# The entry of an attention and mixture-of-experts kernel: constant matmuls while TensorE waits, finer waits, and copies moved to ScalarE

## The chip, the cores and the metric

One core of a Trainium2 chip runs the whole program. The metric is the device time of one execution in microseconds (us), lower is better.

## The reference

```
x:  [16, 512, 128] float32          # 16 batches of 512 tokens, 128 wide
xn = layernorm(x)
out = x + attention(xn) + experts(xn)

attention: q, k, v = xn Wq, xn Wk, xn Wv in 16 heads of 8; q and k scaled to length 1 per head
           softmax(8 q k^T, causal) v, then Wo
experts:   8 experts of 128 -> 512 -> 128 with gelu and biases; each token goes to the 2 experts
           with the highest router probability, weighted by those two probabilities made to sum to 1
```

## The kernel before

The program has these stages. **Stage A** (to about 75 us) normalises the 16 batches two at a time, turns them, and has TensorE compute for each token the router's logits and the raw q and k (`joint`); ScalarE squares those (`squares`), GpSimd sums the squares per head (`sum_squares`, L580), ScalarE takes the roots (`roots`, L770), all to scale q and k later. The **entry** (75 to 118 us) routes the tokens and starts attention; it is what the change touches. Then follow attention for batches 0 to 7, the expert tiles, and attention for batches 8 to 15, in which the expert results come back.

**Attention of one batch** is one `body` per engine, in an order written out by hand. TensorE goes through 12 units k (`scores`, L892): each fills 1536 columns of scores in one of two sets of three PSUM banks. ScalarE takes the exponential of each unit in one instruction (L812) into `prob`; TensorE may fill unit k+1 of scores only when the exponential of unit k-1 is done. GpSimd cuts off the causal part (`mask`, L657). TensorE weighs the values with the result in ten chunks (`weigh`, L926), five per half of the heads, into the one PSUM bank `ps_o` (bank 6); VectorE empties it with `evacuate` (L1349) after chunk 4 and after chunk 9. Chunk 5 waits for the first emptying.

**The next batch is prepared inside this one.** For each of the four 128-token tiles of batch b+1, TensorE computes q, k and v (`project`, L870, into bank 7), and VectorE runs `prepare`: `unload` scales q and k into `qn` and copies v (L1229), `halve` splits q and k into a 16-bit high part and remainder in `dup` (L1238, L1240) and copies both parts once more (L1245, L1246). When `dup_done` counts the tile, SP issues a DMA transpose into `qks` (`turn_qk`, L431). The first scores of a batch wait for all four transposes. TensorE can't project the next tile before VectorE has copied v of the last (`proj_evac`).

**Batch 0's own tiles** are prepared in the entry, into banks 0 to 3. `project(0, 2)` and `project(0, 3)` wait until ScalarE has read the last of the raw q and k.

**Routing.** VectorE's `select` finds the first and second expert of each token (`selected`). TensorE counts them with matmuls against ones and a residue mask (L985 to L994), and ranks every token in `ps_pc`, bank 7 (L997, L999; `placed`). VectorE turns counts into where each expert's rows begin, in some twenty small dependent steps, gives the position of the padding (`pad_ready`), turns ranks into slots and then counts `routed`:

```
            dve.memset(ps_o, 0.0).then_inc(r_step, 1)
            dve.wait_ge(r_step, next_step())
            dve.sem_inc(routed, 1)
```

Three places wait for `routed`: TensorE before `project(1, 0)` (it writes bank 7, where the ranks are) and before `weigh(0, 0, 0)` (it writes bank 6, where the counts are), and GpSimd before it moves the first rows to their slots. GpSimd's part of batch 0 is: first the indirect DMA that writes the padding rows (`pad_last_tiles`, L620, waits for `pad_ready`), then the masks, and from unit 5 on, once `routed` and the padding's landing (`padded`) are there, eight indirect DMAs (`move`, L650) spread over the masks of units 5 to 10.

SP's queue in the entry holds, in order: the transposes of batch 0, two loads of rows, the load of `xt` for batch 1, and the load of half of `acc` (2 MB).

ScalarE's order in the entry is: the last 8 `squares`, the last six roots (batches 10 to 15), the exponentials. GpSimd's sum for batch b waits until the roots of batch b-2 are taken, since `sums` has two buffers.

## Time and profile before

| | |
|---|---|
| median of 3 runs | 680.59 us (680.46 to 680.67) |
| the profiled execution's own time | 680.41 us |
| its span | 678.7 us |
| busy TensorE / VectorE / ScalarE / GpSimd | 615.8 / 465.7 / 449.9 / 418.0 us |
| mean granted TensorE clock | 0.975 of full |

The profile is of one execution; its times count from the start of the span. PE is TensorE, PEld its loading of weights, DVE VectorE, ACT ScalarE, POOL GpSimd, SPq SyncE's DMA queue. In the timeline a row merges instructions of one line that follow each other: start, us, engine, line, operation, how many, and in brackets the idle time before it and what ended it. The granted clock is 1.00 at 2.4 GHz and 0.50 at 1.2 GHz. "Issue" is idle time that ended with nothing the profile shows as a releaser.

### The profile page before, as it was taken

How to read it: one execution, taken by the hardware profiler on the slowest of the kernel's cores; microseconds unless marked ns; L12 is line 12 of the kernel's file. 1: busy time of each engine (PE TensorE's matmuls, PEld its weight loads, DVE VectorE, ACT ScalarE, POOL GpSimd, SP SyncE). 2: the span in 40 equal slices, each digit the busy share in tenths (PEclk: the TensorE clock that was granted, in tenths of full speed). 3: DMA queues.
4: the chain of work that ended last, by engine and by line, in shares of the span. 5: the costliest groups of instructions: out<-in, count | busy, mean ns of one | idle time of the engine just before them, and what ended most of it. 6: DMA issues, size and time to landing. Idle time of an engine off the chain costs nothing. (4 is left out here: it accounts for less than half of the span.)

```text
span 678.7 us, 21454 instructions
## 1 busy us (share of the span) xinstructions
PE 615.8 (91%) x7417; PEld 411.7 (61%) x7417; DVE 465.7 (69%) x1312; ACT 449.9 (66%) x689; POOL 418.0 (62%) x584
## 2 busy tenths in 40 slices
PE   2877558999999999999999999999999999999965
PEld 2755323444444438999999999999984444444423
DVE  7799986766676776445545446777566687878826
ACT  3999546888888884444444444444449888888854
POOL 6355627778777787775600027677737777677771
PEclk9899968999999999999999999999999999999989
DMA  5997685655445578855432335444536375556621
GB/s 160 297 288 228 185 248 111 109 108 104 115 115 118 125 126 199 206 143 143 108 88 71 73 88 120 112 115 118 120 78 104 84 137 116 121 124 139 122 68 32
DMA packets 186592, 89.36 MB, mean 132 GB/s; under 512 B 115456, under 2 KB 176032, under 8 KB 186400
## 3 DMA queue, kind: packets, MB, share of 16 engines
q1 hardware_dynamic: 178192, 70.70, 44.7%
q0 software_dynamic: 8336, 17.84, 9.8%
q8 instruction: 36, 0.59, 0.4%
q14 instruction: 28, 0.23, 0.1%
HBM read 30.17 MB, written 32.24 MB: 92 GB/s over the span
## 5 line engine op out<-in xcount | busy, mean ns | idle before, releaser
L812 ACT ACTIVATE prob<-psum 128x1536 f32<-128x1536 f32 x192 | 267.2, 1453 | 64.0 <-PE psum L922 62.2
L822 ACT ACTIVATE prob<-psum,prob 128x256 f32<-128x256 f32 x284 | 117.5, 471 | 132.2 <-PE psum L1062 129.3
L648 POOL DMA_INDIRECT rows<-slot_y,idx x128 | 130.4, 1019 | 46.1 <-issue 27.2
L650 POOL DMA_INDIRECT slot_x<-rows,slots x128 | 128.2, 1001 | 36.1 <-issue 30.4
L954 PE MATMUL psum<-prob,v 128*18 128x448 f32 (+3 forms) x2048 | 137.9, 388 | 8.6 <-POOL prob L664 8.6
L664 POOL TENSOR_SCALAR_AFFINE_SELECT prob<-prob 128x384 f32<-128x384 f32 (+2 forms) x224 | 104.8, 477 | 62.6 <-ACT prob L812 60.5
L1074 PEld LDWEIGHTS psum<-prob 128*128 128x128 f32 x1136 | 137.8, 192 | 3.6
L1074 PE MATMUL psum<-prob 128*128 128x128 f32 x1136 | 138.1, 275 | 0.0
L1062 PE MATMUL psum<-xs,prob 128*128 128x256 f32 x568 | 134.8, 380 | 0.6 <-DVE xs L1468 0.4
L1062 PEld LDWEIGHTS psum<-xs,prob 128*128 128x128 f32 x568 | 102.5, 190 | 12.4 <-DVE xs L1468 0.6
L954 PEld LDWEIGHTS psum<-prob,v 128*18 128x18 f32 x2048 | 48.8, 98 | 97.0 <-issue 75.9
L922 PE MATMUL psum<-qks 32*128 32x192 f16 (+3 forms) x1024 | 74.2, 276 | 2.5 <-ACT prob L812 2.4
L1475 DVE TENSOR_TENSOR xs<-psum,prob 128x256 f32<-128x256 f32 x71 | 30.1, 425 | 52.5 <-PE psum L1074 52.5
L882 PE MATMUL psum<-wall,xt 128*128 128x384 f32 x128 | 58.5, 541 | 3.6 <-issue 3.1
L1452 DVE COPY prob<-wexp 128x516 f32 x71 | 31.4, 443 | 38.0 <-ACT prob L822 34.6
L922 PEld LDWEIGHTS psum<-qks 32*128 32x128 f16 x1024 | 22.1, 92 | 42.4 <-ACT prob L812 17.4
L1460 DVE COPY prob<-wexp 128x640 f32 x71 | 35.8, 505 | 14.8 <-DVE xs L1475 14.5
L1397 DVE SCALAR_TENSOR_TENSOR acc<-rows,gate,acc 128x128 f32<-128x128 f32 (+1 forms) x128 | 42.7, 398 | 1.4 <-DVE acc L1381 0.8
L633 POOL COPY idx<-slots 128x8 int32 (+1 forms) x16 | 3.7, 231 | 63.8 <-PE psum L1074 63.6
L1240 DVE TENSOR_TENSOR dup<-qn,dup 128x256 f16<-128x256 f32 x64 | 36.3, 567 | 2.2
L1222 DVE TENSOR_TENSOR qn<-psum,rnb 128x256 f32<-128x256 f32 x36 | 14.8, 412 | 31.1 <-PE psum L882 31.0
L845 PE MATMUL psum<-wall,xts 128*128 128x264 f32 x128 | 32.3, 399 | 4.2 <-ACT logits L767 4.2
(159 smaller groups left out, 661.3 us busy)
## 6 DMA issues: line engine op xcount, KB each, us to landing
slot_y<-xs SPq DMA_DIRECT2D x71, 128.0 KB
xs<-in_L_attn_x SPq DMA_DIRECT2D x16, 256.0 KB, 4.1
prob<-in_L_ffn_W SPq DMA_DIRECT2D x16, 256.0 KB, 3.6
xn_rows<-prob SPq DMA_DIRECT2D x16, 256.0 KB, 2.7
xn_cols<-xts SPq DMA_DIRECT2D x16, 256.0 KB, 3.0
xt<-xn_cols SPq DMA_DIRECT2D x16, 256.0 KB
rows<-xn_rows SPq DMA_DIRECT2D x16, 256.0 KB, 3.5
out<-acc SPq DMA_DIRECT2D x15, 256.0 KB
```

Source lines behind the costliest of these rows:

```text
L648: pool.indirect_dma_start(rows[:, j, c, t, :], None, done, where).then_inc(moved[j], 16)
L650: pool.indirect_dma_start(slot_x, where, halves_of_rows[:, j, 0, t, :], None).then_inc(moved[j], 16)
L664: pool.affine_select(out=p, in_=p, compare_op=ALU.is_ge, fill=0.0, base=HP, pattern=[[0, n], [0, 2], [1, HP]], channel_multiplier=-1).then ...
L812: act.activation(prob[:, KEPT[k], :], score[k % 2], ACT.Exp, scale=SCALE / UP ** 2)\
L822: act.activation(hs[:, s, c, :], psum[:, 2 * s + c // 2, (c % 2) * FT:(c % 2 + 1) * FT], ACT.Gelu, bias=ws[:, s, B1C + c:B1C + c + 1]).the ...
L882: pe.matmul(bank[:, 0:3 * D], xt[:, t * P:(t + 1) * P], wall[:, E:WEND], start=True, stop=True)\
L922: mm = pe.matmul(s[:, j * N + col:j * N + col + cols], keys, queries(qks[g:g + 32, par, 0, slab], kt, first, cols), start=True, stop=True)
L954: mm = pe.matmul(queries(ps_o[32 * g:32 * g + VW], kt, first, cols), pairs[par][:, kt * H // 2 + QH * o + g, odd:odd + VW], prob[:, KEPT[u ...
L1062: mm = pe.matmul(psum[:, 2 * s + c // 2, (c % 2) * FT:(c % 2 + 1) * FT], ws[:, s, c * P:(c + 1) * P], xgt[:, s, :], start=True, stop=True)
L1074: mm = pe.matmul(psum[:, 4 + s, j * D:(j + 1) * D], hs[:, s, c, j * P:(j + 1) * P], ws[:, s, W2C + c * D:W2C + (c + 1) * D], start=(c == 0 ...
L1240: dve.tensor_tensor(dup[:, t, :, :, 3 * DH:4 * DH], whole_qk, dup[:, t, :, :, 0:DH], ALU.subtract)\
L1397: dve.scalar_tensor_tensor(out=a, in0=r, scalar=gate[:, c, at(TB * m + t)], in1=a, op0=ALU.mult, op1=ALU.add).then_inc(combined, 1)
```

## The change

In seven parts:

1. TensorE: 24 matmuls of the constant `identh` with the constant `barred` (512 columns each) into bank 7, whose result nobody reads, before the wait for `selected`; six more into a bank of scores after the last weighing of batch 0.
2. TensorE: batch 0 has an order of its own, `first_batch`. `weigh(0, 0, 0)` comes after unit 3 instead of 4, the projections of batch 1 after units 4, 8, 9 and 11 instead of 3, 5, 7 and 8. The first two units of scores stand, as before, behind the ranks.
3. `routed` is split: `counts_read` releases `weigh(0, 0, 0)`, `ranks_read` releases `project(1, 0)`, and `routed` is left to GpSimd alone. VectorE's memset of `ps_o` goes.
4. ScalarE takes from VectorE, for batch 0, the copy of v and the two copies within `dup` (`share_first`): 12 instructions.
5. ScalarE takes the roots of batches 10 and 11 ahead of the last squares, and those of 12 to 15 between and behind its copies.
6. VectorE: the bias copy stands ahead of the last selection instead of behind it, `share_values(0, 0)` ahead of the counts; in batch 0 `evacuate(0, 0)` stands ahead of tile 2 of batch 1 instead of behind all tiles and `pick_tiles`.
7. GpSimd: the padding's DMA stands behind the masks of units 0 and 1 instead of ahead of them.

```diff
@@ gpsimd, body
-                if known(b, 0):
-                    pad_last_tiles()
                 for k in range(UN):
                     mask(b, k)
+                    if known(b, 0) and k == 1:
+                        pad_last_tiles()
@@ scalar
             stage_a(act, step)
+            roots(NB // 2 - 3)
             for s in range(2):
                 squares(NB // 2 - 1, 1, s)
-            for i in range(NB // 2 - 3, NB // 2):
-                roots(i)
+
+            def share_first(t):
+
+                act.wait_ge(qn_done, t + 1)
+                to = v[:, 0, t * H:(t + 1) * H, 0:DH].rearrange("p (m j) d -> p j m d", j=2)
+                act.copy(to, psum[:, t, 2 * D:3 * D].rearrange("p (j m d) -> p j m d", j=2, d=DH)).then_inc(proj_evac, 1)
+                act.wait_ge(lo_done, t + 1)
+                q_to = dup[:, t, 0].rearrange("p h (c d) -> p h c d", d=DH)
+                k_to = dup[:, t, 1].rearrange("p h (c d) -> p h c d", d=DH)
+                act.copy(q_to[:, :, 1:3, :], q_to[:, :, ::-3, :])
+                act.copy(k_to[:, :, 1:3, :], k_to[:, :, ::3, :]).then_inc(dup_done, 1)
+            act.wait_ge(made, 3)
+            for t in range(TB):
+                share_first(t)
+                if t < 2:
+                    root(NB - 4 + t)
+            for b in range(NB - 2, NB):
+                root(b)
@@ tensor, project
                     if i == 0 and known(b, 1):
-                        pe.wait_ge(routed, 1)
+                        pe.wait_ge(ranks_read, 1)
@@ tensor, weigh
                     if known(b, 0):
-                        pe.wait_ge(routed, 1)
+                        pe.wait_ge(counts_read, 1)
@@ tensor, entry
+            def keep_going(bank, n):
+
+                pattern = barred[:].rearrange("p (a c) -> p a c", a=1).broadcast_to([P, 2 * TB, HP])
+                for _ in range(n):
+                    pe.matmul(bank, identh[:], pattern, start=True, stop=True)
+            keep_going(ps_pc, 24)
             pe.wait_ge(selected, T // ST)
...
             pe.wait_ge(proj_evac, TB)
+            scores(0, 0, 0)
+            scores(0, 0, 1)
+
+            def first_batch():
+
+                for k in range(2, UN):
+                    scores(0, 0, k)
+                    if k == 3:
+                        weigh(0, 0, 0)
+                    elif k == 4:
+                        project(1, 0)
+                    elif k in (5, 6, 7):
+                        weigh(0, 0, k - 4)
+                    elif k == 8:
+                        project(1, 1)
+                    elif k == 9:
+                        weigh(0, 0, 4)
+                        project(1, 2)
+                    elif k == 10:
+                        weigh(0, 0, 5)
+                        weigh(0, 0, 6)
+                    elif k == 11:
+                        project(1, 3)
+                        weigh(0, 0, 7)
+                        pe.wait_ge(exp_done, UN - 1)
+                        keep_going(score[0][:, 0:N], 6)
@@ vector, unload and halve, batch 0
+                if known(b, 0):
+                    return
...
+                if known(b, 1) and i == 0:
+                    dve.wait_ge(dup_done, TB)
@@ vector, entry
-            for c in range(TOPK):
-                select(T // ST - 1, c)
             dve.wait_ge(btr_done, 1)
             dve.tensor_copy(wexp[:, :, B1C:W2C], psum[:, 5, 0:E * MC].rearrange("p (e c) -> p e c", e=E))\
                 .then_inc(bt_ready, 1)
+            for c in range(TOPK):
+                select(T // ST - 1, c)
+            share_values(0, 0)
...
             stepped(dve.tensor_copy(counts[:], ps_o[:, 0:2 * E].rearrange("p (c e) -> p c e", c=2)))
+            dve.sem_inc(counts_read, 1)
...
             stepped(dve.tensor_tensor(at_rank, ranks, of_halves(begins[:, 0:2]), ALU.add))
+            dve.sem_inc(ranks_read, 1)
...
-            dve.memset(ps_o, 0.0).then_inc(r_step, 1)
-            dve.wait_ge(r_step, next_step())
             dve.sem_inc(routed, 1)
@@ vector, body
                     prepare(b + 1, 1 - par, 1, second)
+                    if known(b, 0):
+                        evacuate(0, 0)
                     prepare(b + 1, 1 - par, 2, second)
```

How the instructions stand now, at three places. First TensorE in batch 0, from unit 3 of scores on (`qks` are scores, `wall,xt` a projection, `prob,xts` the weighing of chunk 0). Before:

```order
L922 MATMUL psum<-qks 128x448 [waits exp_done]
L922 MATMUL psum<-qks 128x448 x2
L922 MATMUL psum<-qks 128x64 x3
L882 MATMUL psum<-wall,xt 128x384 [waits proj_evac,routed,xt_in]
L922 MATMUL psum<-qks 128x320 [waits exp_done]
L922 MATMUL psum<-qks 128x320 x2
L922 MATMUL psum<-qks 128x192 x3
L943 MATMUL psum<-prob,xts 18x64 [waits exp_done,vp_ready,routed,proj_evac]
L943 MATMUL psum<-prob,xts 18x64 x15
```

And now:

```order
L944 MATMUL psum<-qks 128x448 [waits exp_done]
L944 MATMUL psum<-qks 128x448 x2
L944 MATMUL psum<-qks 128x64 x3
L965 MATMUL psum<-prob,xts 18x64 [waits exp_done,vp_ready,counts_read,proj_evac]
L965 MATMUL psum<-prob,xts 18x64 x15
L944 MATMUL psum<-qks 128x320 [waits exp_done]
L944 MATMUL psum<-qks 128x320 x2
L944 MATMUL psum<-qks 128x192 x3
L904 MATMUL psum<-wall,xt 128x384 [waits proj_evac,ranks_read,xt_in]
```

The weighing has moved ahead of unit 4, the projection behind it, and neither names `routed`. Second, TensorE at the end of batch 0, from unit 11 on, where nothing but a weighing stood between these scores and the next batch's first row (`barred,identh` waiting for the transposes):

```order
L944 MATMUL psum<-qks 128x320 [waits exp_done]
L944 MATMUL psum<-qks 128x320 x2
L944 MATMUL psum<-qks 128x192 x3
L904 MATMUL psum<-wall,xt 128x384 [waits proj_evac]
L976 MATMUL psum<-prob,v 18x448 [waits masked]
L976 MATMUL psum<-prob,v 18x448 x3
L976 MATMUL psum<-prob,v 18x64 x4
L1009 MATMUL psum<-barred,identh 128x512 [waits exp_done]
L1009 MATMUL psum<-barred,identh 128x512 x5
L928 MATMUL psum<-barred,identh 128x512 [waits qk_turned3,qk_turned2,exp_done,qk_turned1,qk_turned0]
```

The last projection of batch 1 now stands behind the last unit of scores, and the six constant matmuls behind the weighing. Third, ScalarE between its last square and its first exponential, where before only six roots stood:

```order
L812 COPY v<-psum 128x2x8x8 [waits qn_done,made]
L816 COPY dup<-dup 128x16x16 [waits lo_done]
L817 COPY dup<-dup 128x16x16
L778 ACTIVATE norms<-rows 128x128 [waits ss_ready]
L812 COPY v<-psum 128x2x8x8 [waits qn_done]
```

Each tile's three copies come in this order, the roots of batches 12 and 13 behind tiles 0 and 1.

## Rows read from the trace of the kernel before

**Rows 1.** The page, part 1: busy time and share of the span.

```profile
PE 615.8 (91%) x7417; PEld 411.7 (61%) x7417; DVE 465.7 (69%) x1312; ACT 449.9 (66%) x689; POOL 418.0 (62%) x584
```

**Rows 2.** Stretches: length, busy us (count) of PE, PEld, DVE, ACT, POOL; PEclk; DMA; GB/s.

```profile
80.00:82.00 2.00, 0.00 (x0) 0.00 (x0) 1.90 (x6) 0.31 (x1) 1.73 (x3) 0.96 0.94 232
...
94.00:96.00 2.00, 0.60 (x12) 0.12 (x6) 1.90 (x4) 2.00 (x2) 1.62 (x3) 0.87 1.05 289
...
112.00:114.00 2.00, 1.06 (x36) 1.01 (x40) 1.93 (x5) 1.16 (x1) 1.69 (x3) 0.64 0.91 173
...
118.00:138.00 20.00, 19.45 (x353) 8.51 (x343) 14.48 (x37) 16.87 (x12) 14.38 (x23) 1.00 0.58 110
```

**Rows 3.** Timeline of ACT, batches 0, 1 and 8: start, us, engine, line, operation [idle before].

```profile
92.31 5.48 ACT L812 ACTIVATE prob<-psum 128x1536 f32<-128x1536 f32 x4 [6.89 <-PE psum L922]
...
118.43 5.48 ACT L812 ACTIVATE prob<-psum 128x1536 f32<-128x1536 f32 x4 [0.75 <-PE psum L922]
...
509.52 10.93 ACT L812 ACTIVATE prob<-psum 128x1536 f32<-128x1536 f32 x8 [3.28 <-PE psum L922]
...
525.51 1.45 ACT L812 ACTIVATE prob<-psum 128x1536 f32<-128x1536 f32 x1 [0.25 <-PE psum L922]
```

**Rows 4.** Waits of PE, 60 to 125: total us, times, longest.

```profile
PE psum L985 <- DVE gap L1135: 9.6, 1, 9.6
...
PE psum L882 <- issue: 3.1, 1, 3.1
...
PE psum L943 <- DVE turn L1355: 2.5, 1, 2.5
```

**Rows 5.** Timeline of DVE, 72 to 87.

```profile
72.69 0.42 DVE L1222 TENSOR_TENSOR qn<-psum,rnb 128x256 f32<-128x256 f32 x1
...
81.62 1.14 DVE L1121 TENSOR_TENSOR mark<-logits,top 128x128 f32<-128x128 f32 x1
...
84.77 0.29 DVE L1121 TENSOR_TENSOR mark<-spent,top 128x128 f32<-128x128 f32 x1
...
86.28 0.17 DVE L1135 TENSOR_TENSOR gap<-top 128x16 f32<-128x16 f32 x1
```

**Rows 6.** Timeline of DVE and POOL in batch 0.

```profile
100.59 0.42 DVE L1222 TENSOR_TENSOR qn<-psum,rnb 128x256 f32<-128x256 f32 x1
...
102.05 0.22 DVE L1246 COPY dup<-dup 128x256 f16<-128x256 f16 x1
...
104.77 0.98 POOL L650 DMA_INDIRECT slot_x<-rows,slots  x1 [0.25 <-issue]
```

**Rows 7.** Timeline of PE, 75 to 118.

```profile
75.15 1.56 PE L882 MATMUL psum<-wall,xt 128*128 128x384 f32 x4 [0.53 <-ACT logits L767]
...
76.64 0.24 PE L980 MATMUL psum<-identf,b1n 32*128 32x32 f32 x1
...
90.17 1.06 PE L906 MATMUL psum<-barred,identh 128*128 128x512 f16 x2
...
113.77 1.93 PE L954 MATMUL psum<-prob,v 128*18 128x448 f32 x16
...
117.09 0.60 PE L906 MATMUL psum<-barred,identh 128*128 128x512 f16 x2
```

**Rows 8.** Timeline of ACT and POOL, 64 to 76.

```profile
64.95 1.05 ACT L757 COPY prob<-xns 128x1024 uint16<-128x1024 uint16 x1
...
73.77 0.39 ACT L766 ACTIVATE prob<-psum 128x256 f32<-128x256 f32 x1
...
75.45 0.40 POOL L601 TENSOR_TENSOR rows<-rows 128x128 f32<-128x128 f32 x1 [3.87 <-ACT norms L773]
```

**Rows 9.** DMA issues, 60 to 125: KB each, us to landing.

```profile
qks<-dup SPq DMA_TRANSPOSE x9, 3.6
...
acc<-in_L_attn_x SPq DMA_DIRECT2D x1, 0.5 KB, 11.8
...
slot_x<-acc,pad_at POOLq DMA_INDIRECT x1, 7.8
```

More of the change, by code:

```diff
@@ L253, in build @@
         r_step, counted, totals_read, placed = sems("r_step counted totals_read placed")
-        routed = sem("routed")
+        routed, counts_read, ranks_read = sems("routed counts_read ranks_read")
         residue_ready, later_ready = sems("residue_ready later_ready")
@@ L774, in roots, with root @@
                         .then_inc(norms_ready, 1)
+            def root(b):
+                act.wait_ge(ss_ready, b + 1)
+                act.activation(norms[:, TB * b:TB * (b + 1), :], sums[:, b % 2], ACT.Sqrt, scale=1.0 / UP ** 2)\
+                    .then_inc(norms_ready, 1)
             def step(i, par, j):
@@ L1019, in body @@
                         if not last:
[L1020 removed]
+                            project(b + 1, 1)
                     elif k == 4:
```

26 lines of the change are left out of this document (13 added, 13 removed).

## The prediction

> **What bounds the kernel now.** I read the page first: TensorE is busy for 91% of the span [rows 1], so most of the program is out of reach of an edit to its entry. The table by stretches shows the same for a settled stretch of attention: 19.45 of 20 us at granted clock 1.00, the higher level, 2.4 GHz [rows 2]. The change touches none of that code; it can only move the moment from which this regime runs. So I read the exponentials of ScalarE (one per unit of scores) in the timeline: the first of batch 0 starts at 92.31, the first of batch 1 at 118.43 [rows 3]. Batch 0 thus lasts 26.1 us, while batch 8, which enters with its operands ready, needs 16.0 us from its first to its last exponential [rows 3]. The room is there, and before it.
>
> TensorE's waits name three holes [rows 4]: 9.6 us for `selected` (VectorE's top-2 selection), 3.1 us before a projection ("issue": it is the wait for `routed`, the end of VectorE's routing), and 2.5 us for VectorE to empty the accumulator of batch 0. In their wake the granted clock is at or falls to 0.50, that is 1.2 GHz [rows 2]: the first hole starts at 76.88 [rows 7], and the row of 80 to 82 still has 0.96; the third starts near 110.5, and the row of 112 to 114 has 0.64. All later work is counted from semaphores, none from the clock on the wall, so I take what batch 1 starts earlier as what the program ends earlier.
>
> **Part 1: until `selected`.** The last selection op ends at 86.45 [rows 5]. VectorE loses twelve copies of batch 0, 0.22 to 0.28 us each [rows 6], some 0.7 per tile. Tiles 0 and 1 take from 72.69 [rows 5] to about 75.3 instead of 76.1. Tiles 2 and 3 can't start before their projection, which is behind ScalarE's squares (75.15, 1.56 for two [rows 7]); they end near 79.7 instead of 81.4. With 0.2 for the bias copy, now ahead, selection starts at 80.0 instead of 81.3. The selection itself took 5.1 us because GpSimd was still summing squares: the same comparison costs 1.14 then and 0.29 later [rows 5]. GpSimd loses 3.87 us at 75.45 to a root that ScalarE put behind the squares [rows 8]; the change moves that root ahead and interleaves the next ones, so GpSimd ends its sums about 3.7 us earlier, near 80.0. The selection then takes 4.0, twice the quiet half. `selected`: 84.0, **2.4 earlier**.
>
> The Trainium skill, SBUF — State Buffer, on the shared port pair, says that a GpSimd operation and certain VectorE operations exclude each other for the whole instruction; it agrees in direction with 1.14 against 0.29, but the step above needs only those two rows.
>
> ScalarE takes the copies. A 256-element activation is 0.39 [rows 8]; I take 0.3 + 0.39 + 0.39 = 1.1 per tile, tile 3 done at about 80.7, so its transpose (landing 3.6 after issue [rows 9]) is there at 84.4, before TensorE asks at 87. Bounds for one copy: 0.22, VectorE's own, and 1.05, a 1024-element ScalarE copy [rows 8]; I take 0.39 because size and type are nearest. SP's queue behind the transposes (rows, xt, acc) keeps its order.
>
> **Part 2: from `selected` to the first exponential.** Before: 86.45 to 92.31, 5.9 us, at the low clock. Two bias matmuls show the price of the level: 1.06 at 90.17 against 0.60 at 117.09 [rows 7]. The 24 added matmuls run from 76.9; at 0.27 to 0.30 each (half of that 0.60) they end by 83.4 to 84.1, at most 0.1 after `selected`. At the low level, 0.53 each, they would end at 89.6. The clock is high when they start (0.96 even in 80 to 82 [rows 2]), so I take the first. `share_values`, two copies on VectorE, hides under the counting matmuls. Ranks and first scores at the high clock: 5.9 becomes about 4.3, **1.6 earlier**. First exponential: 88.3.
>
> **Part 3: batch 0.** `weigh(0, 0, 0)` now needs only `counts_read` (about 86.5) and comes after unit 3; `project(1, 0)` needs `ranks_read`, two 512-element ops after the padding position, about 91.7, and is due at 92.8: the 3.1 us hole is gone, no wait takes its place. VectorE finishes routing near 95.9, without the memset and with `share_values` already done, and can take tile 0 of batch 1 at 97.2; before it was 100.59 [rows 6]. The evacuation of the first half moves ahead of tiles 2 and 3 and of `pick_tiles`, so TensorE's 2.5 us hole goes too. Exponentials follow batch 8's pace: 16.0 us from first to last.
>
> What is late next is GpSimd. Its padding transfer moves behind the mask of unit 1 (about 92) and took 7.8 us to land, against an acc load in flight that took 11.8 [rows 9]. The acc load now starts some 3 us sooner, so I take 6.5: padded at 98.5, while mask 5 is through at 97.6. Between 97.6 (no wait) and 101 (7.8, and the read in its way again). Then eight moves of 0.98 plus 0.2 to 0.3 [rows 6] and seven masks hold the masks of units 8 and 9 to about 105 and 108; I charge 1.5 us: last exponential at 88.3 + 16.0 + 1.5 = 105.8.
>
> From there the path to batch 1 is: `project(1, 3)`, now only behind unit 11, 0.8 plus 0.1; VectorE's preparation, 100.59 to 102.27 = 1.7 [rows 6]; SP 0.1; landing 3.6 [rows 9]; two bias matmuls and the scores, 117.09 to 118.43 = 1.3 [rows 7, 3]. Sum 7.6, so 113.4 against 118.43 [rows 3]: 5.0 earlier. TensorE meanwhile has one weighing (about 1, half of 1.93 [rows 7]) and the six added matmuls (1.6), then is idle for about 2.3 us; before, it lost the clock after some 2 us of idling (0.64 in 112 to 114 [rows 2]). A fall costs the first scores 0.8 (2.1 instead of 1.3) and up to another 1.0 in a batch in which TensorE has no slack. Nothing to 1.8; I take 1.2.
>
> **Sum:** 5.0 − 1.2 = 3.8 us off the profiled execution's 680.41 gives 676.6; the median of the runs shown is 680.59, 0.18 above it, so I forecast **676.8**. A difference of 0.2%, 1.4 us, is about what a measurement of this kernel can tell.
>
> **Rivals.**
> *No stall and no fall of the clock.* Padding lands before it is asked for and the two charges (1.5 and 1.2) vanish: 680.6 − 6.5 = 674.1. For it: the added matmuls stand exactly in the two largest holes. Against it: the 3.6 us landing behind a late `project(1, 3)` is plain. Chance 0.2.
> *The clock falls again within batch 0.* Right after the dense start, units 2 and 3 leave TensorE 0.4 us of work in each 1.35 us of ScalarE, and the hole around `selected` leaves it idle for 1 to 2 us. In the trace such a stretch was followed by a fall (0.87 in 94 to 96 [rows 2]). It would cost first the ranks and scores (1.6, the gain of part 2), later the weighings, 1.93 a chunk at the low level [rows 7], of which half would be saved at the high one, some 1 us more: 676.8 + 2 = 678.8, up to 679.6. Chance 0.25.
> The Trainium skill, TensorE: Matmul & The Clock Gate, A second HAM failure mode, says that a TensorE that idles briefly between groups of matmuls swings between the two levels. That rule speaks against batch 0 keeping the clock, as this rival has it; the sum without the rule is 676.8, with it 678.8.
> *Gain is taken back downstream* (GpSimd's moves or SP's loads set the start of batch 1 or 2, whatever VectorE does): within 1.4 us of 680.6. For it: eight moves are issued in batch 0 on the same engine as the masks. Against it: TensorE is full to 19.45 in 20 us from 118 on [rows 2], so it, and not GpSimd, sets the pace there. Chance 0.06.
> *Slower: ScalarE's copies.* They are strided, half from the 16-bit tile. The queue is ScalarE's: two of the last roots, then the table load and the first exponential stand behind them, and SP's transposes, with the acc load behind those. At 1.05 each, twelve copies and two roots end at 75.0 + 13.2 = 88.2; the last transpose lands at 91.9, the first exponential is at 93.4, 1.1 late; the acc load starts near 91 and shares the padding's time (97 + 11.8, the longest landing seen), so mask 9 is at 118 and batch 1 starts at about 120.5: 682.5. It decides from about 0.95 us per copy on. Chance 0.06.
>
> **The numbers.** My forecast, 0.43; no stall 0.2; clock falls 0.25; taken back 0.06; slower 0.06. The range reaches from the no-stall case, 674.1, to the worst of the falling clock, 679.8. Faster by over 0.2% (below 679.2): 0.43 + 0.2 + most of 0.25 = 0.86; same 0.07, slower 0.07.
>
> **What would show it.** `selected` near 84 with comparisons of 0.3 us; the 24 matmuls over by then; granted clock 1.00 through 76 to 92; first exponential at 88.3; no "issue" wait before a projection; GpSimd's first move at 98 to 99; first exponential of batch 1 at 113 to 115. The forecast is wrong if ScalarE's copies exceed 0.6 us, if the row around 84 to 90 reads 0.50, if padding holds GpSimd to 101, or if batch 2 starts less early than batch 1 does.

## The result, and the profile after

The changed kernel takes **684.91 us** (median of 14 runs, 680.88 to 688.09); the kernel before, on the same chip, 680.76 us (14 runs, 680.04 to 682.39). The ratio is 1.0055, 95% interval 1.0034 to 1.0077: slower by half a per cent, where 0.6% faster was forecast. The profiled execution is the slowest of the 14, 688.09 us with a span of 685.3, against 680.41 and 678.7 before; a place that it shows as late need not be as late in the median run.

The page, part 1, of the changed kernel [rows 1]:

```profile
PE 629.8 (92%) x7447; PEld 416.4 (61%) x7447; DVE 464.0 (68%) x1299; ACT 452.9 (66%) x701; POOL 416.6 (61%) x584
```

TensorE is busy 14.0 us longer, though the 30 added matmuls are only 5.35 + 1.47 us of it.

ScalarE's timeline, its first copies and the exponentials [rows 3]:

```profile
75.88 0.43 ACT L816 COPY dup<-dup 128x256 f16<-128x256 f16 x1
...
91.68 6.82 ACT L834 ACTIVATE prob<-psum 128x1536 f32<-128x1536 f32 x5 [6.83 <-PE psum L944]
...
110.58 1.45 ACT L834 ACTIVATE prob<-psum 128x1536 f32<-128x1536 f32 x1 [1.69 <-PE psum L944]
118.14 1.45 ACT L834 ACTIVATE prob<-psum 128x1536 f32<-128x1536 f32 x1 [6.12 <-PE psum L944]
...
140.37 2.79 ACT L834 ACTIVATE prob<-psum 128x1536 f32<-128x1536 f32 x2 [0.76 <-PE psum L944]
```

Batch 0 starts 0.63 us earlier than before, batch 1 0.29 earlier (118.14 against 118.43), batch 2 already 2.0 **later** (140.37 against 138.34), and from batch 2 to the end of the span it takes 544.9 instead of 540.4 us. 2.0 + 4.5 is the whole difference of the spans (6.6), and in this execution most of it arises in code that the change does not touch. (The two executions differ by 7.7 us; the other 1.1 lies outside the spans.)

Stretches of the changed kernel [rows 2]:

```profile
80.00:82.00 2.00, 2.00 (x11) 0.92 (x10) 1.83 (x4) 0.88 (x3) 1.86 (x4) 1.00 0.93 317
...
86.00:88.00 2.00, 0.78 (x11) 0.52 (x12) 1.54 (x6) 0.00 (x0) 0.00 (x0) 0.86 0.91 207
88.00:90.00 2.00, 2.00 (x6) 0.71 (x5) 1.60 (x11) 0.00 (x0) 0.00 (x0) 0.50 1.03 306
...
96.00:98.00 2.00, 2.00 (x16) 0.64 (x8) 1.77 (x4) 2.00 (x2) 1.94 (x3) 0.50 1.00 313
...
118.00:120.00 2.00, 2.00 (x38) 0.75 (x36) 0.00 (x0) 1.45 (x1) 0.28 (x1) 0.54 0.00 0
...
118.00:138.00 20.00, 20.00 (x291) 8.03 (x289) 12.73 (x36) 15.63 (x11) 12.36 (x20) 0.83 0.49 91
...
630.00:632.00 2.00, 2.00 (x37) 1.13 (x36) 0.00 (x0) 1.78 (x2) 0.43 (x2) 0.54 0.03 8
```

TensorE's timeline [rows 7]:

```profile
77.56 5.35 PE L1009 MATMUL psum<-barred,identh 128*128 128x512 f16 x24
86.40 0.40 PE L1014 MATMUL psum<-ones,both 128*128 128x128 f16 x4 [3.49 <-DVE gap L1190]
...
89.89 1.06 PE L928 MATMUL psum<-barred,identh 128*128 128x512 f16 x2
...
110.46 0.91 PE L904 MATMUL psum<-wall,xt 128*128 128x384 f32 x2
112.24 1.06 PE L976 MATMUL psum<-prob,v 128*18 128x448 f32 x16 [0.86 <-POOL prob L664]
113.23 1.47 PE L1009 MATMUL psum<-barred,identh 128*128 128x512 f16 x6
116.82 0.59 PE L928 MATMUL psum<-barred,identh 128*128 128x512 f16 x2 [2.12 <-issue]
```

The 24 constants run at the high level, 0.22 us each, and are over at 82.9. Then TensorE has nothing until 86.40, the clock falls to 1.2 GHz near 87.3, and the ranks and bias matmuls run at the old price (1.06). It is low again in 94 to 100, during batch 0. The waits for routing and for the first emptying are gone. The last projection starts at 110.46; the last exponential of batch 0 at 110.58, where before it was 116.22. But batch 1 can't start before the last tile's transpose, and from 110.58 to 118.14 pass 7.6 us; of these 2.12 are a hole behind the six constants. Right behind it the clock falls, and batch 1 runs its first 6 us at the low level: 22.23 us instead of 19.91.

VectorE and GpSimd, timeline of the changed kernel [rows 5, 8, 6]:

```profile
78.44 1.28 DVE L1295 CAST dup<-qn 128x256 f16<-128x256 f32 x1
...
82.42 0.28 DVE L1174 TENSOR_REDUCE top<-logits 128x16 f32<-128x128 f32 x1
82.73 0.29 DVE L1176 TENSOR_TENSOR mark<-logits,top 128x128 f32<-128x128 f32 x1
...
86.18 0.17 DVE L1190 TENSOR_TENSOR gap<-top 128x16 f32<-128x16 f32 x1
...
78.30 1.27 POOL L594 TENSOR_TENSOR rows<-prob 128x512 f32<-128x512 f32 x1 [0.17 <-POOL rows L601]
...
95.53 1.21 POOL L623 DMA_INDIRECT slot_x<-acc,pad_at  x1 [0.47 <-issue]
...
102.57 0.98 POOL L650 DMA_INDIRECT slot_x<-rows,slots  x1 [1.61 <-issue]
```

and the same pair before:

```profile
76.64 0.80 DVE L1238 CAST dup<-qn 128x256 f16<-128x256 f32 x1
...
76.02 1.27 POOL L594 TENSOR_TENSOR rows<-prob 128x512 f32<-128x512 f32 x1 [0.17 <-POOL rows L601]
```

GpSimd did end its sums earlier (80.8 instead of 83.8), and the selection behind them is quick (0.29 a comparison). But the same sums now start almost with VectorE's casts. A cast takes 0.28 alone; here it ends 0.15 us after the sum does, whenever it began: before at 77.44 against 77.29, now at 79.72 against 79.57. The first selection step is at 82.42, not at 80.0.

### The profile page after: what moved, and what is told of

It is laid out like the page before. It is cut to its first block and busy times, and to the rows that moved or that the text cites. A ratio compares the mean times of both kernels' runs of the same rounds, so it can differ in the third digit from the quotient of the medians.

```text
span 685.3 us, 21517 instructions
## 1 busy us (share of the span) xinstructions
PE 629.8 (92%) x7447; PEld 416.4 (61%) x7447; DVE 464.0 (68%) x1299; ACT 452.9 (66%) x701; POOL 416.6 (61%) x584
## 5 line engine op out<-in xcount | busy, mean ns | idle before, releaser
L664 POOL TENSOR_SCALAR_AFFINE_SELECT prob<-prob 128x384 f32<-128x384 f32 (+2 forms) x224 | 103.4, 471 | 78.5 <-ACT prob L834 64.6
L976 PE MATMUL psum<-prob,v 128*18 128x448 f32 (+3 forms) x2048 | 139.9, 393 | 10.6 <-POOL prob L664 10.4
L1129 PEld LDWEIGHTS psum<-prob 128*128 128x128 f32 x1136 | 137.8, 192 | 3.6
L944 PE MATMUL psum<-qks 32*128 32x192 f16 (+3 forms) x1024 | 75.6, 280 | 2.8 <-ACT prob L834 2.7
L904 PE MATMUL psum<-wall,xt 128*128 128x384 f32 x128 | 60.0, 554 | 0.5 <-ACT logits L767 0.5
```

The lines of the kernel that those rows point to most:

```text
L664: pool.affine_select(out=p, in_=p, compare_op=ALU.is_ge, fill=0.0, base=HP, pattern=[[0, n], [0, 2], [1, HP]], channel_multiplier=-1).then ...
L904: pe.matmul(bank[:, 0:3 * D], xt[:, t * P:(t + 1) * P], wall[:, E:WEND], start=True, stop=True)\
L944: mm = pe.matmul(s[:, j * N + col:j * N + col + cols], keys, queries(qks[g:g + 32, par, 0, slab], kt, first, cols), start=True, stop=True)
L976: mm = pe.matmul(queries(ps_o[32 * g:32 * g + VW], kt, first, cols), pairs[par][:, kt * H // 2 + QH * o + g, odd:odd + VW], prob[:, KEPT[u ...
L1129: mm = pe.matmul(psum[:, 4 + s, j * D:(j + 1) * D], hs[:, s, c, j * P:(j + 1) * P], ws[:, s, W2C + c * D:W2C + (c + 1) * D], start=(c == 0 ...
```

## The experiments

All times are medians of 6 to 14 runs, beside runs of the kernel before on the same chip; its median there was 679.7 for a1 to a4 and 680.2 to 680.8 for the others. The ratio and its interval are against those runs; the ratio is an estimate of its own and differs from the quotient of the medians by up to 0.3%. From each profile I take three starts, the first exponentials of batches 0, 1 and 2 (b0, b1, b2), and "rest", the span minus b2. These come from one execution each, which can be far from the median: d4's profile is 7.3 us below it, c3's 2.1 below, c4's 2.2 and the changed kernel's 3.2 above. "Added" is the number of TensorE matmuls more than before; each is two instructions, a weight load and a matmul. No kernel leaves out part of the computation; the constant and small matmuls write what nobody reads. The theories are numbered in the order in which I formed them: **theory 5** is that the number of added instructions moves the loading of TensorE's instructions against the later batches; **theory 6** that the padding's transfer shares its time with the `acc` load and so holds GpSimd's first move and batch 0.

| kernel | added | b0 | b1 | b2 | rest | median | ratio (95%) |
|---|---|---|---|---|---|---|---|
| before | 0 | 92.31 | 118.43 | 138.34 | 540.4 | 680.8 | |
| changed | 30 | 91.68 | 118.14 | 140.37 | 544.9 | 684.9 | 1.0055 (1.0034–1.0077) |
| a1_no_constant | 0 | 91.29 | 118.76 | 141.12 | 541.4 | 683.8 | 1.0052 (1.0030–1.0074) |
| a2_end_16 | 40 | 92.05 | 121.37 | 141.28 | 543.4 | 684.5 | 1.0064 (1.0041–1.0087) |
| a3_start_38 | 44 | 89.69 | 120.32 | 142.49 | 552 | 686.4 | 1.0093 (1.0057–1.0129) |
| a4_project_early | 30 | 92.09 | 117.87 | 137.79 | 543.4 | 683.9 | 1.0056 (1.0033–1.0078) |
| b1_pad_first | 30 | 91.36 | 117.60 | 137.51 | 544.9 | 686.0 | 1.0098 (1.0080–1.0116) |
| b2_pad_project | 30 | 91.55 | 118.14 | 138.05 | 543.5 | 684.4 | 1.0063 (1.0046–1.0081) |
| b3_copies_back | 30 | 93.11 | 119.63 | 139.54 | 542.8 | 685.5 | 1.0104 (1.0066–1.0141) |
| b4_before_split | 0 | 92.89 | 119.46 | 139.37 | 538.6 | 678.7 | 0.9973 (0.9952–0.9993) |
| c1_before_30 | 30 | 92.59 | 119.00 | 138.91 | 545.4 | 684.3 | 1.0053 (1.0031–1.0076) |
| c2_before_128 | 128 | 92.59 | 118.81 | 138.72 | 540.1 | 680.3 | 0.9989 (0.9976–1.0003) |
| c3_after_128 | 128 | 91.71 | 120.44 | 139.69 | 541.7 | 685.2 | 1.0062 (1.0042–1.0082) |
| c4_project_128 | 128 | 90.11 | 121.09 | 141.01 | 540.5 | 681.1 | 1.0004 (0.9989–1.0019) |
| d1_split_late_acc | 0 | 92.62 | 119.18 | 139.03 | 540.5 | 679.7 | 0.9981 (0.9959–1.0003) |
| d2_project_128_late | 128 | 89.14 | 112.49 | 132.38 | 540.3 | **675.9** | 0.9932 (0.9912–0.9953) |
| d3_project_none_late | 0 | 92.05 | 116.28 | 138.95 | 540.7 | 681.8 | 1.0020 (1.0006–1.0034) |
| d4_after_late_acc | 30 | 91.27 | 116.56 | 136.47 | 542.3 | 687.8 | 1.0124 (1.0102–1.0147) |
| e1_project_late_30 | 30 | 92.10 | 116.72 | 136.63 | 545.2 | 682.7 | 1.0031 (1.0008–1.0054) |
| e2_after_128_late | 128 | 89.68 | 115.85 | 138.70 | 539.2 | 678.4 | 0.9979 (0.9961–0.9997) |

Read the column "rest" first. With 0 or 128 added it is 538.6 to 541.7 in ten profiles, with 30 it is 542.3 to 545.4 in eight, with no overlap; with 40 (a2) it is 543.4. (a3's profile, 696.35 us, lies 10 us above its median, and its row is not used for this.)

One place separates the kernels more sharply than "rest" does. Batch 13 lasts 19.0 to 20.0 us in the ten profiles with 0 or 128 added, and 20.8 to 21.5 in the ten with 30, 40 or 44 (a3's counted here). TensorE's idle time just before batch 14 is at most 0.92 us in the first ten and 1.76 to 2.26 in the others.

Of the expectations below, those of b4, c1, c2, e1 and e2 were met in the median, and d2's within 0.1 us. The medians of a2 to a4, b1, b2, c3, c4, d1, d3 and d4 fell outside what the theory under test gave; those of a1 and b3 decide little.

**Constants: none, more at the end, more at the start.**

```diff
@@ a1_no_constant
-            keep_going(ps_pc, 24)
-                        pe.wait_ge(exp_done, UN - 1)
-                        keep_going(score[0][:, 0:N], 6)
@@ a2_end_16
-                        keep_going(score[0][:, 0:N], 6)
+                        keep_going(score[0][:, 0:N], 16)
@@ a3_start_38
-            keep_going(ps_pc, 24)
+            keep_going(ps_pc, 38)
```

> The changed kernel without its 24 + 6 constant matmuls. Theory 1 (the loss is the fall of TensorE's clock at the start of batch 1, which lasts 22.2 us instead of 19.9): without the six the idle stretch before batch 1 is longer still, the clock falls there or before, batch 1 starts no later; about the same as the changed kernel, 684 to 687. Theory 2 (the constant matmuls themselves hold up work): faster than the changed kernel by over 1 us.

> The changed kernel with 16 instead of 6 constant matmuls behind the last weighing of batch 0, so that TensorE is busy until the transposes of batch 1 have landed. Theory 1 (fall of the clock): batch 1 runs at 1.00 and lasts about 19.9 us instead of 22.2, the median falls by 2 us or more, to 682 or 683, and the runs scatter less. Rival (the start of batch 1 is bound by something else and the clock costs nothing): no change, or up to 1 us slower where the ten added matmuls outlast the transposes.

> The changed kernel with 38 instead of 24 constant matmuls ahead of the selection (about 8.5 us instead of 5.4, from 77.5 to 86.0, with selected at 86.3). If the clock that fell at 87.3 is what kept the first exponential at 91.7, it starts at about 90.2 now and batch 1 up to 1.5 us earlier: 683 to 684. If the start of batch 1 is bound by the late projection and GpSimd's masks, the first exponential moves and batch 1 does not.

Without constants "rest" is 3.5 shorter and b2 0.75 later, and the median is 683.8, as good as with them: they gain nothing where they stand. It also shows that the changed kernel is slower than the one before (1.0052) without a single added matmul; of the 3.8 us between those two spans, 2.8 lie ahead of batch 2. Sixteen at the end bridge the wait for the transposes, and batch 1 keeps its clock (19.91 us), but batch 0 is longer and the sum is no better. Thirty-eight at the start reach `selected`, and b0 comes 2 us earlier; batch 0 then takes 30.6 us instead of 26.5. That is from the profile set aside above, but c4 shows the same in an ordinary one (31.0). Something else held batch 0.

**The projections of batch 1 earlier; the padding's DMA first; both.**

```diff
@@ a4_project_early
                     elif k in (5, 6, 7):
                         weigh(0, 0, k - 4)
+                        if k == 7:
+                            project(1, 1)
                     elif k == 8:
-                        project(1, 1)
-                    elif k == 9:
                         weigh(0, 0, 4)
                         project(1, 2)
                     elif k == 10:
+                        project(1, 3)
                         weigh(0, 0, 5)
                         weigh(0, 0, 6)
                     elif k == 11:
-                        project(1, 3)
                         weigh(0, 0, 7)
@@ b1_pad_first
+                if known(b, 0):
+                    pad_last_tiles()
                 for k in range(UN):
                     mask(b, k)
-                    if known(b, 0) and k == 1:
-                        pad_last_tiles()
@@ b2_pad_project: both
```

> The changed kernel with the projections of tiles 1, 2 and 3 of batch 1 after units 7, 8 and ahead of the chunks of unit 10 (instead of after units 8, 9 and 11), and weighing of chunk 4 after unit 8. Theory 2 (batch 1 starts late because its last tile is projected behind the last unit of scores, at 110.5): the last transpose is issued 2 to 3 us earlier, TensorE's idle time before batch 1 goes, batch 1 starts at about 116 and keeps the clock: 681 or less. Theory 1 alone gives the same gain by the clock. Rival (GpSimd's masks behind its moves set the end of batch 0): no change.

> The changed kernel with the padding's DMA back ahead of the mask of unit 0. Theory 3 (GpSimd sets the end of batch 0: its first row move waits for the padding to land, 102.5 in the changed kernel, and the masks of units 7 to 9 stand behind the moves): padding is issued at 93 instead of 95.5, the first move stands at 100 to 101, batch 1 starts 1.5 to 2 us earlier, and, as TensorE idles less before it, may keep its clock: 681 to 683. Rival (late projection, theory 2): first move earlier, batch 1 unchanged, 684 to 685.

> Both the padding first and the projections early. If both bounds count, batch 1 starts about 3 us before the 118.1 of the changed kernel, near 115, and lasts 19.9: 680 to 681. If one of them is the bound, no better than the better of the two alone.

With the last projection behind unit 10 the hole before batch 1 is filled and b2 is at 137.8, 2.6 us before the changed kernel's, yet the median moves by 1 us: "rest" is still 543.4. Issuing the padding first gains nothing: its landing goes from 6.3 to 9.1 us, and the first move comes at 102.2 instead of 102.6. Together they are no better.

**ScalarE's copies and roots undone; the split of the waits alone.** b3 is the changed kernel with the last six roots behind the squares, and VectorE's 12 copies back. b4 is the kernel before with only parts 3 and 6 of the change (less the reordering of `evacuate` and the bias copy):

```diff
@@ b4_before_split
-                        pe.wait_ge(routed, 1)
+                        pe.wait_ge(ranks_read, 1)
...
-                        pe.wait_ge(routed, 1)
+                        pe.wait_ge(counts_read, 1)
...
+            share_values(0, 0)
             dve.wait_ge(btr_done, 1)
...
-            dve.memset(ps_o, 0.0).then_inc(r_step, 1)
-            dve.wait_ge(r_step, next_step())
```

> The changed kernel with the twelve copies of batch 0 back on VectorE and the roots back behind the squares. Theory 4 (the earlier roots put GpSimd's sums beside VectorE's casts, so these cost 1.28 instead of 0.28, and moving copies gains nothing before selected): selected no later than in the changed kernel, time the same. If moving the copies did gain the 0.8 us that the trace shows against the last squares, selected is that much later and the time 0.5 to 1 us more.

> The kernel before with only the split of the routing's wait (counts, ranks), share_values ahead of the counts and no memset. TensorE's 3.1 us wait before the first projection goes. If that wait was on the path, batch 0 is shorter by up to 3 us and the time is 678 to 679. If the landing of the padding (101) takes its place, since GpSimd then reaches unit 5 before it, batch 0 is shorter by 1 to 2 us at most: within 1 us of the kernel before.

b3's `selected` is late by what the copies had gained:

```profile
87.25 0.61 PE L997 MATMUL psum<-ones,both 128*128 128x128 f16 x4 [4.35 <-DVE gap L1173]
```

0.85 us after 86.40, and b0 1.4 later; the median is 0.5 us above the changed kernel's, and the ratio 1.0104 against 1.0055, with intervals that overlap. So parts 4 and 5 do no harm; whether they help in the total is not shown. The split alone is the first version that is faster than before, by 0.27%, and its "rest" is not longer.

**The number of instructions by itself.** The kernel before, with small matmuls in its 9.6 us wait for `selected`:

```diff
@@ c1_before_30 (c2_before_128: 128)
+            for _ in range(30):
+                pe.matmul(psum[0:32, 7, 0:HP], identh[:, 0:32], barred[:], start=True, stop=True)
             pe.wait_ge(selected, T // ST)
@@ c3_after_128, the changed kernel (c4_project_128: the same on a4)
-            keep_going(ps_pc, 24)
+            keep_going(ps_pc, 20)
+            for _ in range(102):
+                pe.matmul(psum[0:32, 7, 0:HP], identh[:, 0:32], barred[:], start=True, stop=True)
```

> The kernel before with 30 small matmuls (32 weights columns, 64 columns, result unread) in TensorE's 9.6 us wait for the selection; they take some 1 to 2 us of it. Theory 5 (the change's 30 added matmuls, 60 instructions with their weight loads, shift where the later program's instruction fetches, 16 KB each in the DMA rows, fall, so that some fall beside the transposes at a batch's end and cost up to 2 us more where the clock then falls): the time from the start of batch 2 to the end rises from 540.4 by 2 us or more, as in every kernel that holds the constant matmuls (542.8 to 552), with batch 2 at 20.2 or more instead of 19.46 and batch 13 at 20.8 or more instead of 19.78; median 682 or more. Rival (the later losses of the changed kernel come from when batch 1 starts, or from ScalarE's and GpSimd's order): 680.2, within 0.5, like the kernel before.

> The same with 128 small matmuls: 256 instructions of 64 bytes, just one fetch of 16 KB. Theory 5: every later fetch falls where it did, one further on, so from batch 2 on as in the kernel before (540.4), batches 2 and 13 at 19.5 and 19.8; median within 1 us of before, or a little faster as the clock falls later in the wait. Rival (any added matmuls cost later): as the one with 30.

> The changed kernel with 20 + 102 small + 6 = 128 added matmuls instead of 24 + 6. Theory 5: from the start of batch 2 on 540.4 instead of 544.9; the entry unchanged or up to 1 us later: 681 to 682. Rival: 684 to 686 as the changed kernel.

> The same in the kernel with the projections early, whose batch 2 began at 137.8 (1.3 us earlier than in the kernel before, counted from the last squares). Theory 5: 679 to 680, beating the kernel before by about 1 us. Rival: 683 to 684 as without it.

These runs show what the count does to the kernel before. Thirty matmuls, 1.05 us of work hidden in a wait of 9.6, make the old kernel **3.5 us slower**, 1.0053, near the ratio of the whole change. A hundred and twenty-eight of them, 3.91 us of work in the same wait, cost nothing. The fetching of instructions has rows of its own in the DMA part of the page: the larger of two queues named "instruction" has 36 packets, 0.59 MB, so 16 KB each, and I take it to be TensorE's. How many instructions one carries I can only estimate. Ten intervals between fetches span the 73 us from 117 to 190 in the kernel before, in which TensorE starts 2,546 loads and matmuls: some 255 for each. The queue then fetches nothing from 190 to 234, from 263 to 499 and from 562 to 607, where the program goes again through loops of two batches or two expert tiles. That 256 is a whole number of pieces was a guess that led to the run, and the fetches agree with it. From 117 to 190 they fall into the microseconds 117, 125, 132, 138, 146 before, and into 117, 126, 132, 139, 147 with 128, which has one more fetch, at 81, in the wait itself; with 30 it is 115, 122, 129, 137, 146. Around batch 8, whose first exponentials are at 509.52, 509.57 and 510.92, they fall into 510, 517 and 526 before and with 128 as well, but into 510, 517 and 527 with 30, against the batch some 1.4 us earlier at the first two. c1 loses 0.4 us in batch 2 (19.85 against 19.46), 0.8 in batch 8, 1.5 in batch 13 and 2.4 in batch 14, where nothing was changed.

Where part of it is lost can be seen at the end of batch 13. Timeline of SP and TensorE, the last transpose's issue and the next batch's first matmul. Before:

```profile
619.69 1.24 SPq L431 DMA_TRANSPOSE qks<-dup  x1
...
624.72 0.59 PE L906 MATMUL psum<-barred,identh 128*128 128x512 f16 x2 [0.73 <-ACT prob L812]
```

c2, with 128:

```profile
619.25 1.24 SPq L431 DMA_TRANSPOSE qks<-dup  x1
...
624.21 0.59 PE L906 MATMUL psum<-barred,identh 128*128 128x512 f16 x2 [0.67 <-ACT prob L812]
```

c1, with 30:

```profile
621.58 1.24 SPq L431 DMA_TRANSPOSE qks<-dup  x1
...
627.91 0.59 PE L906 MATMUL psum<-barred,identh 128*128 128x512 f16 x2 [2.00 <-issue]
```

and the changed kernel:

```profile
622.43 1.23 SPq L431 DMA_TRANSPOSE qks<-dup  x1
...
628.50 0.59 PE L928 MATMUL psum<-barred,identh 128*128 128x512 f16 x2 [1.80 <-issue]
```

From issue to first row 5.0 and 5.0 us without or with 128, 6.3 and 6.1 with 30. TensorE idles 2.0 and 1.8 us instead of 0.7. In these two kernels the clock then falls: the stretch 630 to 632 above has 0.54 and batch 14 takes 22.2 us in the changed kernel and 21.7 in c1, against 19.3 and 19.4. But the wait is not enough for the fall. a2 waits longest of all but one, keeps 1.00, and its batch 14 takes 19.4; a4, b2, b3 and d4 keep it too, after 1.76 to 2.13 us. Timeline and stretch of a2:

```profile
630.76 0.59 PE L928 MATMUL psum<-barred,identh 128*128 128x512 f16 x2 [2.25 <-issue]
```

```profile
632.00:634.00 2.00, 2.00 (x40) 0.82 (x38) 0.00 (x0) 1.92 (x2) 0.34 (x2) 1.00 0.14 41
```

Shown is that the loss hangs on the count, and that a part of it arises in the wait ahead of batch 14, where the program asks for the transposes. What lengthens the wait is not shown. That an instruction fetch delays the transpose was my inference, and the traces do not bear it out. Behind the issue of the last transpose the larger instruction queue fetches after 4.3, 2.7, 3.2 and 2.5 us (before, c2, c1, changed), which does not set the slow pair apart. The packets of the hardware DMA queue run off alike before and in c1: 3.3 us behind the issue 8,641 and 8,602 are still to come. Only the changed kernel lags, with 8,700. A rival that I did not test is that TensorE itself runs short of instructions there: its idle time ends with "issue" in both late kernels, that is with nothing that the profile shows as a releaser.

c3 and c4 have "rest" back at 541 and still don't win: their batch 0 takes 28.7 and 31.0 us. c4's median is 2.8 us below a4's, but c3's, 685.2, is the changed kernel's own, and is where the rival had put it: in the order of the changed kernel the right count alone gains nothing. Part of why is in c3's profile. Its constants end 1.30 us before the ranks, and the clock falls all the same, so that the ranks cost 1.91 and b0 is no earlier (91.71):

```profile
86.44 0.40 PE L1016 MATMUL psum<-ones,both 128*128 128x128 f16 x4 [1.30 <-DVE gap L1192]
...
88.22 1.91 PE L1030 MATMUL psum<-turn,xs 128*128 128x512 f16 x4
```

c4, timeline of GpSimd and its DMA landings:

```profile
105.98 0.98 POOL L650 DMA_INDIRECT slot_x<-rows,slots  x1 [6.87 <-issue]
```

```profile
acc<-in_L_attn_x SPq DMA_DIRECT2D x1, 0.5 KB, 17.2
slot_x<-acc,pad_at POOLq DMA_INDIRECT x1, 11.2
```

The earlier `selected` brings padding and `acc` load together: 11.2 us to land instead of 6.3, and GpSimd stands still for 6.87. That is theory 6.

**The `acc` load behind the loads for batch 2.** SP issues it after the `xt` of batch 2, instead of in the entry:

```diff
@@ d1 to d4, e1, e2
-            load_acc(0, T // 2)
...
                         load_xt(b + 2)
+                    if known(b, 0):
+                        load_acc(0, T // 2)
```

d1 is b4 with it, d2 is c4, d3 is a4 without any constants, d4 is the changed kernel; e1 is a4 with its 30 constants, e2 is c3.

> The kernel before with the split waits, share_values ahead, no memset, and the load of half of acc behind the transposes and the xt load of batch 0's body. Theory 6 (padding behind the acc load bounds batch 0 once the waits are split): padding lands in 4 to 6 us, the first move stands at 100 or before instead of 103.4, batch 1 starts 1 to 2 us earlier than 119.5: 677 to 678. Rival (batch 0 there is bound by TensorE at the low clock): as the split alone, 678.7.

> The changed kernel with early projections, 128 added matmuls and the late acc load. Theory 5 and 6: first move at 98 to 100 instead of 106, batch 0 24 to 25 us instead of 31, batch 1 at 115 to 116, from batch 2 on 540.4: 676 to 677.5. If only theory 5 holds, 681 as without the late load.

> The same with no constant matmuls at all. Fetches in place as in the kernel before; what is missing is only the clock they keep. Theory: the first exponential 0.5 to 1.5 us later than in the one with 128, batch 1 possibly at the low clock (22 instead of 19.9): 677 to 680.

> The changed kernel with only the late acc load. Theory 6: first move at 99 to 100 instead of 102.6, batch 1 about 2 us earlier; theory 5: from batch 2 on still 543 to 545: 682 to 683. Rival to theory 5 (the later loss comes from something the late entry causes): back to 679.

> The changed kernel with the projections of batch 1 earlier and the acc load behind batch 2's xt, with its 24 + 6 constant matmuls and none added to make them 128. It differs from the fastest version so far (675.9, 128 added matmuls) only in that number. Theory of the instruction count: the entry is as good as that one's (batch 2 starts within 1 us of 132.4 minus what four more constants in the entry give or take), but from batch 2 to the end it takes 542 to 545 instead of 540.3, so the median is 679 to 683. Rival, that the 128 matter only by keeping TensorE busy in the entry: batch 2 starts 3 to 5 us later, and from batch 2 to the end it takes 540 to 541. Rival, that the count does not matter at all: 675 to 677.

> The changed kernel with its own order of projections, 128 added matmuls (20 constants, 102 small, 6 constants) and the acc load behind batch 2's xt. It differs from the fastest version so far only in the order of projections. Theory: batch 0 is 1 to 3 us longer than that one's 23.35, because the last projection stands behind unit 11, TensorE waits 2 us for the transposes behind the six constants and batch 1 begins at the low clock (22 instead of 19.9); from batch 2 to the end 540 to 542; median 678 to 681. Rival, that the order of projections is worth nothing once the number of instructions is right and the padding lands early: 675 to 677.

**d2 beats both kernels, 675.9 us.** It differs from c4 in the `acc` load alone: the padding lands in 4.8 us, batch 0 goes from 31.0 to 23.4. Timeline of d2, ScalarE, TensorE and GpSimd:

```profile
89.14 10.85 ACT L835 ACTIVATE prob<-psum 128x1536 f32<-128x1536 f32 x8 [5.33 <-PE psum L945]
...
112.49 5.48 ACT L835 ACTIVATE prob<-psum 128x1536 f32<-128x1536 f32 x4 [4.19 <-PE psum L945]
...
80.91 3.15 PE L1013 MATMUL psum<-barred,identh 128*32 128x64 f16 x102
85.35 0.40 PE L1017 MATMUL psum<-ones,both 128*128 128x128 f16 x4 [1.29 <-DVE gap L1193]
...
86.95 1.02 PE L1031 MATMUL psum<-turn,xs 128*128 128x512 f16 x4
87.81 0.59 PE L929 MATMUL psum<-barred,identh 128*128 128x512 f16 x2
...
98.55 0.98 POOL L651 DMA_INDIRECT slot_x<-rows,slots  x1 [0.57 <-issue]
```

TensorE works until 84.1, its idle time is 1.29 instead of 3.49, and ranks and bias matmuls run at the high level (1.02 and 0.59 against 1.91 and 1.06). Every stretch that I read from 82 to 120 is at 1.00:

```profile
88.00:90.00 2.00, 2.00 (x71) 0.95 (x70) 1.76 (x11) 0.86 (x1) 0.00 (x0) 1.00 0.84 256
...
96.00:98.00 2.00, 2.00 (x38) 0.72 (x30) 1.77 (x4) 2.00 (x2) 1.08 (x2) 1.00 0.65 262
...
118.00:120.00 2.00, 1.65 (x46) 0.96 (x46) 1.93 (x7) 1.54 (x2) 1.55 (x3) 1.00 1.05 290
```

The other five take one part away each:
- **The count (e1: 30 for 128).** 682.7, 6.8 more. The profiled spans differ by 9.1: "rest" 545.2 against 540.3 is 4.9 of it, the rest of it is a b2 4.25 later, since 24 constants end 3.51 us before `selected` and the ranks run at the low level. e1 changes both at once, the count and how far the wait is covered, and both parts show.
- **The order of the projections (e2).** 678.4, 2.5 more. Its batch 1 starts behind a hole of 2.11 us, at the low clock (1.01 for two bias matmuls instead of 0.59), and takes 22.85 us.

```profile
113.70 1.01 PE L929 MATMUL psum<-barred,identh 128*128 128x512 f16 x2 [2.11 <-issue]
```

- **All matmuls (d3).** 681.8, 5.9 more: "rest" is as good (540.7), but b0 is 2.9 later and batch 1 is at the low clock (22.7).
- **The `acc` load (c4).** 681.1, 5.2 more. Against e2, c3 has 685.2.
- **The `acc` load helps only then.** On the split alone it does nothing (d1 0.9981, b4 0.9973), though the padding lands in 4.8 there too (and in 8.7 in b4). On the changed kernel itself (d4) the median is 687.8, not better but worse; its profile is its fastest run (680.5), so the place of that loss was not seen.

## Why the prediction was wrong

**The step that failed** is the one on which the whole sum stands: "All later work is counted from semaphores, none from the clock on the wall, so I take what batch 1 starts earlier as what the program ends earlier." The later work is the same but does not take the same time: from batch 2 to the end it took 544.9 us instead of 540.4 in the changed kernel's profile, and thirty idle matmuls ahead of it cost the kernel before 3.5 us by themselves (c1), while 128 cost nothing (c2). No term of mine stood for the number of instructions, the range ended at 679.8 (the rival that set it at 679.6), and no rival had it. How the number acts, through the instruction fetches or otherwise, stays open.

The term that this step was to carry on, the start of batch 1 5.0 us earlier, failed as well: batch 1 starts 0.29 earlier, and b2 is 2.0 later, so even with "rest" at 540.4 the kernel would have been slower. This part is enough for a slower kernel by itself: a1 has no added matmul and c3 has 128, and their medians, 683.8 and 685.2, are no better than the changed kernel's. Of the four signs of a wrong forecast that the prediction names, three came: the row from 88 to 90 reads 0.50, padding holds GpSimd beyond 101, and batch 2 starts less early than batch 1. By steps:
- **Part 1, `selected` at 84.0.** 86.40. The copies cost 0.25 to 0.43 as taken (0.39), and the selection 3.9 as taken (4.0). Wrong was its start, 82.42 instead of 80.0: "interleaves the next ones, so GpSimd ends its sums about 3.7 us earlier" moved the sums onto VectorE's casts, 1.28 instead of 0.28. I had priced the shared time only where it was to vanish. 0.7 of the 2.4 is that in this execution the projections came at 75.89 instead of 75.15.
- **Part 2, 1.6 from the clock.** 0.22 us a constant, not 0.27 to 0.30, and `selected` late: the constants ended 3.5 us short of it, and the clock fell. "The clock is high when they start" is right and is not enough. In d2, with the wait filled to 1.3 us, from `selected` to b0 pass 3.8 us (85.35 to 89.14) where I forecast 4.3, so the mechanism can work; in c3, with the same filler and 1.30 us left, the clock fell all the same.
- **Part 3.** The three holes are gone, as forecast. The padding's 6.5 us were 6.3, the first move 102.57 because everything before it was 3.4 late. First to last exponential 18.9 instead of 17.5. The path from there to batch 1 was forecast at 7.6 and measured 7.6.
- **The charge of 1.2 for a fall at the end.** The fall came with batch 1, and cost 2.3 (22.23 against 19.91) in place of "up to another 1.0".

Of the rivals, the clock that falls again within batch 0 came true (0.50 at 96 to 98), and was priced too low, since it also fell in batch 1 and in batch 14. The rule quoted with it, from the Trainium skill, TensorE: Matmul & The Clock Gate, A second HAM failure mode, pointed the right way: the trace agrees that the clock swings where TensorE idles between stretches of work. It gives no price, though, and 678.8, the sum with it, was still 6 us short; and five profiles idle as long ahead of batch 14 without a fall. The rival "slower: ScalarE's copies" fails on 0.43 against its 0.95. The rule on the shared port pair (the Trainium skill, SBUF — State Buffer), which I quoted as agreeing "in direction" only, deserved a term: the trace agrees with it to 0.15 us, as the casts end with the sum.

Open stays what lengthens the wait ahead of batch 14 when 30 matmuls are added, what decides whether the clock falls behind such a wait, and why d4 is slower than the changed kernel.

## What to carry to other kernels

A long program can have a hidden neighbour: here the mere number of instructions added in a wait changed the time of code hundreds of microseconds behind it. Before crediting or blaming an edit, run the old kernel with the same number of idle instructions hidden in a wait, and try other numbers; here 30 and 128 separate 1.0053 from 0.9989. Then do the same to the new kernel, since an effect shown on the old one need not be the loss of the new: there 128 gave 1.0062. Filler matmuls that stop short of the end of the wait gained nothing (24 of them), and those that nearly reach it kept the clock in three of the four kernels that had 122 there. They paid only once the next bound was moved too: none of the constants, the earlier projections and the later `acc` load alone made a kernel faster than before, and together, at the right count, they make 0.7%. The plainest part, the split of the waits, gave 0.27% by itself.

## What the runs showed of the hardware

- Thirty small matmuls hidden in a wait cost 3.5 us, in batches 60 to 550 us behind them; 128 cost nothing. In twenty profiles the wait ahead of batch 14 is 1.76 to 2.26 us with 30, 40 or 44 added and at most 0.92 with 0 or 128. How far the runs of one kernel scatter does not follow the count: 6.8 us in c1 and in a1 (none added), 6.7 in d1 (none), 3.2 in d2.
- The larger instruction queue moves 16 KB packets, one for some 255 loads and matmuls in straight code, and none while a loop of two batches or two expert tiles repeats.
- A 128x256 cast on VectorE that starts within a GpSimd sum of 1.27 us ends 0.15 us behind it: 1.28, 0.91 or 0.80 us by when it starts, 0.28 alone.
- An indirect write that lands in 4.8 to 5.2 us with the 2 MB load issued behind it takes 5.5 to 11.2 with the load issued ahead of it; the load takes 12 to 17.
- The length of an idle stretch of TensorE did not decide by itself whether the clock fell to 1.2 GHz behind it. It fell after 3.49, 2.12 and 1.80 us in the changed kernel, after 2.11 in e2 (batch 1) and after 1.30 in c3; it did not after 1.29 to 1.31 in d2, c4 and e2, after 2.09 in c3 (batch 1) or after 2.25 in a2.
